# One pass over quarter slices for the statistics and the recurrence input, and a normalized input that is recomputed instead of spilled

## The chip, the cores and the metric

The kernel runs on the 8 cores of one Trainium2 chip. Each core works on its own half of one of four sequences, and no core talks to another. The metric is the device time of the slowest core, in microseconds. The chip has two dies, with cores 0 to 3 and 4 to 7.

## What is computed

One layer on x of shape (4, 4096, 2048): a layer norm, a linear recurrence with 256 complex states, a gated feed-forward block that a router switches per token, and a residual.

```python
xn = _layernorm(x, axis=-1)                       # (x - mean) / sqrt(var + 1e-5)
# recurrence on xn:
Bu_re = jnp.einsum('btd,nd->btn', x, gB_re)       # the same for Bu_im
new_re = A_re * h_re - A_im * h_im + bu_re        # scan over t, complex A
y = einsum(H_re, C_re) - einsum(H_im, C_im) + D * x
# block on xn:
routed = jax.nn.sigmoid(x @ w_router + b_router) > 0.5
h = x + (rmsnorm(x, norm1_w) @ wv + bv) @ wo
h2 = rmsnorm(h, norm2_w)
mlp = (silu(h2 @ w_gate) * (h2 @ w_up)) @ w_down
g = silu(where(routed, h + mlp, x))
out = x + y * g
```

D = 2048, FF = 5632. A core has T = 2048 tokens of its own (`xT`, transposed: features are rows, tokens are columns) and a second block of 2048 tokens (`xNB`), the first half of its sequence. From `xNB` it needs only the state at the end of the recurrence, as the start value for its own half (times zero for cores that own a first half).

## The kernel before

Everything is laid out with 128 features or states in the partitions and tokens along the free axis. A feature dimension of 2048 is NK = 16 tiles. The program is written out by hand for five engines: `prog[e]` is the order in which engine e runs, `wait` puts a semaphore wait into it, `milestone` a drain that counts its engine's semaphore up, and `fence` makes engines wait for all others and for all DMA semaphores. `op` puts a drain between every two instructions of VectorE, ScalarE and GpSimd. All x tiles are loaded, and all spills stored, by the DMA queue of SyncE, in program order; the weights are loaded by GpSimd's.

The stages, in order (`pmark` names them):

- P0a: small parameters, and the rotation table `R_bf`, built by doubling on VectorE.
- P0stats_own, P0stats_nb: `stats_pass` loads 16 tiles of 128x2048, casts each on VectorE, squares it on ScalarE, and sums over features with one-column matmuls (weights `ones_bf`, or `sw_sb`, two columns in f32 that also give the router's sum). Then row arithmetic on one partition (mean, variance, `Sqrt`, `reciprocal`), and `bcast`, a matmul with `ones1` that spreads a row over 128 partitions, four quarters each, through banks 6 and 7. The own pass also makes `rr1_bc` and the router's `mask_bc`.
- P0bu_nb, P0bu_own: `bu_pass` loads x again in two halves of 1024 columns, casts on VectorE, and multiplies with `bcat_sb` into four planes of two banks each. Then it applies mean and scale on VectorE. `rotate_scan` rotates the planes by `R_bf` (six tensor operations for each of NG = 2 groups) and runs `tensor_tensor_scan` over 2048 columns. For `xNB` this follows at once; for the own tokens it is `lru_tail_own`, which is called after phase3(0), with the copy into `g_bf`.
- Then, for each half s of the own tokens (1024 columns): `phase3` (x again, `h1_pl`, then v = h1 wv), `phase4` (v wo plus the normalized x gives h, the second norm), `phase5` (gate and up, FFC = 44 steps), `phase6` (down, y, and the output).

In phase4 each of 16 steps d loads `xb4` (one buffer), subtracts `m_bc` and multiplies by `r_bc` into `x4tmp`, stores `x4tmp` to `xnspill` by SyncE's queue, and adds the result of 32 matmuls into `h_pl[d]`. In phase6 each of 16 steps d has two quarters q; each loads h, x and the spilled normalized x (`xn_b`), and VectorE's epilogue runs after the step's matmuls.

The few lines on which most hangs, in `phase4`:

```python
if d >= 1:
    wait("sync", sV, mk_xc[d - 1])
mk_x = dma("sync", sX[0], xb4, xT[d * 128:(d + 1) * 128, c0:c0 + TS])
...
wait("vector", sO, sO.v)
mk_xc[d] = tt("vector", x4tmp, xb4, m_bc[:, c0:c0 + TS], AL.subtract, inc=sV)
mk_xn = tt("vector", x4tmp, x4tmp, r_bc[:, c0:c0 + TS], AL.mult, inc=sV)
wait("sync", sV, mk_xn)
dma("sync", sO, xnsp[d * 128:(d + 1) * 128, c0:c0 + TS], x4tmp)
```

## Time and profile before

| | us |
|---|---|
| two timed runs | 3749.3 and 3793.7, median 3771.5 |
| the profiled execution, device time | 3763.05 |
| its span on the slowest core (core 7) | 3761.5 |
| spans of the other cores | 3733.1 to 3757.8 |

The profile is that of core 7. Its times start at the span's start. The stages of core 7 lie, by the first DMA or the first instruction of each, at 0 to 738 (all of P0), 738 to 928 (phase3(0)), 928 to 1150 (phase4(0)), 1150 to 1778 (phase5(0)), 1778 to 2249 (phase6(0)), 2249 to 2440, 2440 to 2662, 2662 to 3289 and 3289 to the end (the same four for s = 1). TensorE is busy for 73% of the span, VectorE 29%, ScalarE 10%, GpSimd 10%. Busy means an instruction on the engine; the table of stages gives also the granted clock of TensorE (1.00 is 2.4 GHz, 0.50 is 1.2 GHz) and the share of time in which the 16 DMA engines moved data.

### The profile page before, as it was taken

To read this page: it belongs to the slowest core of one execution; us is meant where nothing else is said; L and a number is where in the kernel's file an instruction comes from. 1 tells how busy PE (TensorE), PEld (TensorE's weight loads), DVE (VectorE), ACT (ScalarE), POOL (GpSimd) and SP (SyncE) were. 2 spreads that over 40 slices of the span, in tenths; PEclk is the share of its full clock that TensorE was granted. 3 is DMA by queue.
4 is the path that set the end of the run, shared out by engine and by line. 5 is a ranking of instruction groups with operands and counts; after the bars stand their busy time and mean duration, and the time that the engine had idled before them with its cause. 6 is when DMAs were issued, how large, how long until landed. Compare 5 with 4: busy or idle time off the path is not lost.

```text
span 3761.5 us, 31591 instructions; the slowest of 8 cores (3733.1 to 3761.5 us)
## 1 busy us (share of the span) xinstructions
PE 2757.8 (73%) x11800; PEld 1166.7 (31%) x11800; DVE 1084.0 (29%) x1391; ACT 382.1 (10%) x459; POOL 363.6 (10%) x311
## 2 busy tenths in 40 slices
PE   0635533348856999998688874885599999968887
PEld 0101211113312444444233331332244444423333
DVE  5363455571341101101232333034211010123222
ACT  0212000021111000000000002101200000000000
POOL 0000000001101111111010100110111111101000
PEclk6857676769977999999888986998799999989998
DMA  2404222457957777776787774695777887688876
GB/s 46 142 37 152 92 91 89 111 101 76 153 123 119 79 75 74 76 79 65 122 131 134 124 125 101 69 153 113 135 74 77 79 78 75 63 128 127 138 116 116
DMA packets 749608, 381.71 MB, mean 101 GB/s; under 512 B 684930, under 2 KB 686994, under 8 KB 745362
## 3 DMA queue, kind: packets, MB, share of 16 engines
q0 software_dynamic: 679728, 178.28, 48.8%
q1 hardware_dynamic: 69730, 201.42, 17.0%
q8 instruction: 96, 1.57, 0.2%
q14 instruction: 54, 0.44, 0.0%
HBM read 507.56 MB, written 50.33 MB: 148 GB/s over the span
## 4 chain that ended last, share of the span: by engine, by line
PE 51%; DMA 26%; DVE 14%; issue 4%; ACT 2%; PEld 1%; DVEq 1%; PEldq 1%; SPq 0%; POOL 0%; ACTq 0%; POOLq 0%
PE ps L153 51%; DMA arena<-down_p 9%; DMA arena<-xT 9%; DVE arena L157 7%; DMA arena<-xNB 3%; DVE arena L177 2%; DMA arena<-wv_p 2%; ACT arena L174 2%; DMA arena<-up_p 1%; PEld ps L153 1%; DVE arena L161 1%; PEldq L187 1%; DVEq L121 1%; DVE arena L169 1%; DMA arena<-wo_p 1%
## 5 line engine op out<-in xcount | busy, mean ns | idle before, releaser
L153 PE MATMUL ps<-arena 128*128 128x512 bf16 x11264 | 2566.9, 390 | 691.6 <-DMA arena<-down_p 201.0
L153 PEld LDWEIGHTS ps<-arena 128*128 128x128 bf16 x11264 | 1117.1, 100 | 2143.2 <-issue 910.5
L157 DVE TENSOR_TENSOR arena<-arena,ps 128x512 bf16<-128x512 f32 (+1 forms) x304 | 208.9, 687 | 1760.4 <-ACT arena L174 1127.5
L174 ACT ACTIVATE arena<-arena 128x512 f32<-128x512 f32 (+4 forms) x135 | 146.9, 1088 | 1512.5 <-DVE arena L181 896.5
L174 ACT ACTIVATE arena<-ps 128x512 f32<-128x512 f32 x176 | 105.1, 597 | 1095.5 <-PE ps L153 1082.9
L147 POOL DMA_DIRECT2D arena<-gate_p x88 | 100.6, 1143 | 1163.5 <-PE ps L153 999.4
L157 DVE TENSOR_TENSOR arena<-arena,m_bc 128x1024 f32<-128x1024 f32 x64 | 78.4, 1225 | 423.0 <-DMA arena<-xT 382.1
L157 DVE TENSOR_TENSOR arena<-arena 128x512 f32<-128x512 f32 (+8 forms) x227 | 187.5, 826 | 33.4 <-DMA hspill<-arena 13.0
L153 PE MATMUL ps<-arena,ones_bf 128*1 128x512 bf16 x256 | 82.5, 452 | 152.2 <-ACT arena L174 120.6
L147 POOL DMA_DIRECT2D arena<-down_p x64 | 85.9, 1343 | 788.0 <-PE ps L153 788.0
L177 DVE CAST arena<-arena 128x1024 bf16<-128x1024 f32 (+1 forms) x96 | 83.7, 871 | 254.2 <-DMA arena<-xT 122.2
L147 POOL DMA_DIRECT2D arena<-wv_p x32 | 37.3, 1165 | 1081.0 <-DVEq L187 735.8
L153 PE MATMUL ps<-arena,ones 1*128 1x512 f32 x56 | 50.5, 1075 | 121.6 <-DVEq L187 84.4
L174 ACT ACTIVATE arena<-arena,vp 128x1024 bf16<-128x1024 f32 x64 | 73.4, 1148 | 495.7 <-DVE arena L157 492.5
L147 POOL DMA_DIRECT2D arena<-up_p x88 | 101.2, 1150 | 0.0
L153 PEld LDWEIGHTS ps<-arena,ones_bf 128*1 128x1 bf16 x256 | 19.6, 91 | 216.9 <-issue 209.1
L153 PE MATMUL ps<-arena,sw_sb 128*2 128x512 f32 (+1 forms) x160 | 62.1, 531 | 27.6 <-DMA arena<-xT 26.4
L169 DVE SCALAR_TENSOR_TENSOR arena<-arena,vp,ps 128x512 f32<-128x512 f32 x64 | 47.8, 747 | 59.8 <-ACT arena L174 58.8
L174 ACT ACTIVATE arena<-ps,vp 128x512 bf16<-128x512 f32 x64 | 44.0, 687 | 191.7 <-PE ps L153 186.1
L153 PEld LDWEIGHTS ps<-arena,ones 1*128 1x128 f32 x56 | 16.6, 314 | 150.5 <-issue 150.5
L147 POOL DMA_DIRECT2D arena<-wo_p x32 | 36.5, 1142 | 275.1 <-PE ps L153 243.1
L177 DVE COPY arena<-ps 128x512 f32<-128x512 f32 (+2 forms) x64 | 44.0, 688 | 40.4 <-PE ps L153 33.8
(54 smaller groups left out, 464.8 us busy)
## 6 DMA issues: line engine op xcount, KB each, us to landing
arena<-xT SPq DMA_DIRECT2D x96, 512.0 KB, 5.2
arena<-gate_p POOLq DMA_DIRECT2D x88, 512.0 KB, 7.3
arena<-up_p POOLq DMA_DIRECT2D x88, 512.0 KB, 9.1
arena<-down_p POOLq DMA_DIRECT2D x64, 704.0 KB, 9.6
arena<-xT SPq DMA_DIRECT2D x16, 1024.0 KB, 5.5
arena<-xNB SPq DMA_DIRECT2D x16, 1024.0 KB, 4.9
arena<-xNB SPq DMA_DIRECT2D x32, 512.0 KB, 4.7
arena<-wv_p POOLq DMA_DIRECT2D x32, 512.0 KB, 6.6
```

Source lines behind the costliest of these rows:

```text
L121: prog[e].append(lambda E: E.drain())
L147: return op(queue, lambda E, o=out_ap, i=in_ap: E.dma_start(out=o, in_=i), inc=sem, n=16, is_dma=True)
L153: E.matmul(o, l, r, start=a, stop=b), inc=inc)
L157: E.tensor_tensor(o, a, b, al), inc=inc)
L161: E.tensor_single_scalar(o, a, s, al), inc=inc)
L169: E.scalar_tensor_tensor(o, a, s, b, o0, o1), inc=inc)
L174: E.activation(o, i, f, bias=b, scale=s), inc=inc)
L177: return op(e, lambda E, o=out_ap, i=in_ap: E.tensor_copy(o, i), inc=inc)
L187: em(e, lambda E, h=s.h: E.drain().then_inc(h, 1))
```

## The change

The two statistics passes and the two bu passes over x become one `fused_pass` for `xNB` and one for the own tokens. Each goes over four quarters q of 512 columns; a quarter has 16 steps k. A step loads 128x512 (two buffers), casts and squares on ScalarE, and runs on TensorE: the sum with one f32 column of `sw_sb` (bank 4), for own tokens a second one for the router (bank 6), the sum of squares (bank 5), and four matmuls with `bcat_sb` into banks 0 to 3. After the 16 steps comes the quarter's row arithmetic, now over 512 columns, with `bcq`, a spread through bank 7 alone; ScalarE copies the four planes from PSUM; VectorE applies mean and scale, rotates, and scans, with the last column kept in `small` as the start value of the next quarter. For own tokens ScalarE copies the four results into `g_bf` at each quarter's end. `lru_tail_own` is gone. The order is now xNB first, then own.

In phase4 the store to `xnspill` and its two waits are gone, and the normalized x is made in `h_pl[d]` in place. In phase6 the two loads of it are gone, with SyncE's wait for `mk_Hc`; two tensor operations on 128x512 ahead of each epilogue make it again from the x that is loaded anyway.

The diff, cut to its core (removed bodies of functions are left out, they are printed above):

```diff
--- before.py
+++ after.py
...
-    xnsp = nc.dram_tensor("xnspill", [D, T], F32)
...
     milestone("vector")
...
-    def stats_pass(src, own):
...
-    def bcast(row_ap, dst, qn=4):
...
-    mk_ns = stats_pass(xNB.ap(), False)
...
-    def bu_pass(src, mbc, rbc, mk_ps_free):
...
-    def rotate_scan(init_cols):
...
+    xq2 = [arF(64, 512), arF(66, 512)]
+    xbfq = [arB(68, 512), arB(69, 512)]
+    xsqq = [arB(70, 512), arB(71, 512)]
+    upq = [arF(72, 512), arF(74, 512), arF(76, 512), arF(78, 512)]
...
+    def bcq(row_ap, dst_ap, mk_row):
+        wait("tensor", sV, mk_row)
+        wait("tensor", sV, st["b7"])
+        mk1 = mm(ps[7][:, :], ones1[:, :], row_ap, True, True, inc=sT)
+        wait("vector", sT, mk1)
+        st["b7"] = cp("vector", dst_ap, ps[7][:, :], inc=sV)
+        ps_rd[7] = st["b7"]
+
+    def fused_pass(src, own):
+        mbc_t = m_bc if own else mnb_bc
+        rbc_t = r_bc if own else rnb_bc
+        for q in range(4):
+            cq = q * 512
+            mkB15 = None
             for k in range(NK):
                 sl = k % 2
+                wait("sync", sT, st["S"][sl])
+                wait("sync", sS, st["c"][sl])
+                mk_x = dma("sync", sX[sl], xq2[sl],
+                           src[k * 128:(k + 1) * 128, cq:cq + 512])
+                wait("scalar", sX[sl], mk_x)
+                wait("scalar", sT, st["B"][sl])
+                st["c"][sl] = act(xbfq[sl], xq2[sl], AF.Identity, inc=sS)
+                mk_sq = act(xsqq[sl], xbfq[sl], AF.Square, inc=sS)
+                wait("tensor", sX[sl], mk_x)
+                if k == 0:
+                    wait("tensor", sSm, mk_small)
+                    wait("tensor", sV, st["ev45"])
+                st["S"][sl] = mm(ps[4][0:1, :], sw_sb[:, 2 * k:2 * k + 1],
+                                 xq2[sl], k == 0, k == NK - 1, inc=sT)
+                if own:
+                    if k == 0:
+                        wait("tensor", sV, st["s2e"])
+                        wait("tensor", sV, st["ev6"])
+                    st["S"][sl] = mm(ps[6][0:1, :],
+                                     sw_sb[:, 2 * k + 1:2 * k + 2],
+                                     xq2[sl], k == 0, k == NK - 1, inc=sT)
+                wait("tensor", sS, mk_sq)
+                if k == 0:
+                    wait("tensor", sV, st["ev5"])
+                mm(ps[5][0:1, :], ones_bf[:, :], xsqq[sl], k == 0, k == NK - 1)
+                if k == 0:
+                    wait("tensor", sBc, mk_bcat)
+                    wait("tensor", sS, st["evu"])
                 for pl in range(4):
+                    st["B"][sl] = mm(
+                        ps[pl][:, :],
+                        bcat_sb[:, k * 512 + pl * 128:k * 512 + (pl + 1) * 128],
+                        xbfq[sl][:, :], k == 0, k == NK - 1,
+                        inc=sT if pl == 3 else None)
+                if k == NK - 1:
+                    mkB15 = st["B"][sl]
+            if not own and q == 0:
+                wait("tensor", sV, mk_ones)
+                mk_bs = None
+                for pl in range(4):
+                    for k in range(NK):
+                        mk_bs = mm(ps[6][:, pl:pl + 1],
+                                   bcat_sb[:, k * 512 + pl * 128:
+                                           k * 512 + (pl + 1) * 128],
+                                   negones_bf[:, :], k == 0, k == NK - 1,
+                                   inc=sT if k == NK - 1 else None)
+                wait("vector", sT, mk_bs)
+                for di, c in enumerate((0, 2, 1, 3)):
+                    cp("vector", smc(C_BS + di), ps[6][:, c:c + 1])
+                st["bse"] = milestone("vector")
+            wait("vector", sT, mkB15)
+            st["ev45"] = cp("vector", row2[0:1, cq:cq + 512], ps[4][0:1, :],
+                            inc=sV)
+            st["ev5"] = cp("vector", row_sx2[0:1, cq:cq + 512], ps[5][0:1, :],
+                           inc=sV)
+            if own:
+                st["ev6"] = cp("vector", row_s1[0:1, cq:cq + 512],
+                               ps[6][0:1, :], inc=sV)
+            rm = row2[0:1, cq:cq + 512]
+            rs1 = row_s1[0:1, cq:cq + 512]
+            rsx = row_sx2[0:1, cq:cq + 512]
+            rt = row_tmp[0:1, cq:cq + 512]
+            ra = row_aux[0:1, cq:cq + 512]
+            tsc("vector", rm, rm, INV_D, AL.mult)
+            mk_m = milestone("vector")
+            wait("scalar", sV, mk_m)
+            mk_m2 = act(rt, rm, AF.Square, inc=sS)
+            wait("vector", sS, mk_m2)
+            stt("vector", rsx, rsx, INV_D, rt, AL.mult, AL.subtract)
+            tsc("vector", rt, rsx, 1e-5, AL.add)
+            mk_v = milestone("vector")
+            wait("scalar", sV, mk_v)
+            mk_sq2 = act(rt, rt, AF.Sqrt, inc=sS)
+            wait("vector", sS, mk_sq2)
+            op("vector", lambda E, o=rt: E.reciprocal(o, o))
+            mk_r = milestone("vector")
+            bcq(rm, mbc_t[:, cq:cq + 512], mk_m)
+            bcq(rt, rbc_t[:, cq:cq + 512], mk_r)
+            if own:
+                tsc("vector", ra, rsx, 1e-5, AL.add)
+                op("vector", lambda E, o=ra: E.reciprocal(o, o))
+                tt("vector", ra, rsx, ra, AL.mult)
+                tsc("vector", ra, ra, 1e-6, AL.add)
+                mk_v = milestone("vector")
+                wait("scalar", sV, mk_v)
+                mk_sq2 = act(ra, ra, AF.Sqrt, inc=sS)
+                wait("vector", sS, mk_sq2)
+                op("vector", lambda E, o=ra: E.reciprocal(o, o))
+                tt("vector", ra, ra, rt, AL.mult)
+                mk_rr = milestone("vector")
+                bcq(ra, rr1_bc[:, cq:cq + 512], mk_rr)
+                tsc("vector", ra, rm, small[0:1, C_S2R:C_S2R + 1], AL.mult)
+                tt("vector", ra, rs1, ra, AL.subtract)
+                tt("vector", ra, ra, rt, AL.mult)
+                tsc("vector", ra, ra, br_sb[0:1, 0:1], AL.add)
+                mk_msk = tsc("vector", ra, ra, 0.0, AL.is_gt, inc=sV)
+                bcq(ra, mask_bc[:, cq:cq + 512], mk_msk)
+            wait("scalar", sT, mkB15)
+            wait("scalar", sV, st["car"])
+            mk_ue = None
+            for di, pl in enumerate((0, 2, 1, 3)):
+                mk_ue = act(upq[di], ps[pl][:, :], AF.Identity, inc=sS)
+            st["evu"] = mk_ue
+            wait("vector", sS, mk_ue)
             for di in range(4):
+                stt("vector", upq[di], mbc_t[:, cq:cq + 512], smc(C_BS + di),
+                    upq[di], AL.mult, AL.add)
+                tt("vector", upq[di], upq[di], rbc_t[:, cq:cq + 512], AL.mult)
+            for g in range(NG):
+                Rr = R_bf[:, (2 * g) * T + cq:(2 * g) * T + cq + 512]
+                Ri = R_bf[:, (2 * g + 1) * T + cq:(2 * g + 1) * T + cq + 512]
+                ur, ui = upq[2 * g], upq[2 * g + 1]
+                tt("vector", rAq, ur, Rr, AL.mult)
+                tt("vector", rBq, ui, Ri, AL.mult)
+                tt("vector", rAq, rAq, rBq, AL.subtract)
+                tt("vector", rBq, ui, Rr, AL.mult)
+                tt("vector", ui, ur, Ri, AL.mult)
+                tt("vector", rBq, rBq, ui, AL.add)
+                magc = smc(C_MAG + g)
+                for ri, dsrc in ((0, rAq), (1, rBq)):
+                    i = 2 * g + ri
+                    if q == 0:
+                        ini = smc(C_GI + i) if own else 0.0
+                    else:
+                        ini = smc(C_CAR + i)
+                    op("vector",
+                       lambda E, o=upq[i], d1=dsrc, mc=magc, iv=ini:
+                       E.tensor_tensor_scan(o, mc.broadcast_to([128, 512]), d1,
+                                            iv, AL.mult, AL.add),
+                       inc=sV)
+                    st["car"] = cp("vector", smc(C_CAR + i),
+                                   upq[i][:, 511:512], inc=sV)
+            if own:
+                wait("scalar", sV, st["car"])
+                for i in range(4):
+                    act(g_bf[:, i * T + cq:i * T + cq + 512], upq[i],
+                        AF.Identity)
+                milestone("scalar")
+
+    pmark("P0stats_nb")
+    fused_pass(xNB.ap(), False)
     for g in range(NG):
         pre, pim = smc(28 + 2 * g), smc(28 + 2 * g + 1)
         t1 = smc(C_T1)
-        ge_r = upl[2 * g][:, T - 1:T]
-        ge_i = upl[2 * g + 1][:, T - 1:T]
+        ge_r = smc(C_CAR + 2 * g)
+        ge_i = smc(C_CAR + 2 * g + 1)
         gi_r, gi_i = smc(C_GI + 2 * g), smc(C_GI + 2 * g + 1)
         tsc("vector", gi_r, ge_r, pre, AL.mult)
         tsc("vector", t1, ge_i, pim, AL.mult)
@@ -564,15 +500,17 @@
         tsc("vector", gi_r, gi_r, cmask_sb[:, 0:1], AL.mult)
         tsc("vector", gi_i, gi_i, cmask_sb[:, 0:1], AL.mult)
     milestone("vector")
+    wait("tensor", sS, st["bse"])
+    mk_S2 = None
+    for k in range(NK):
+        mk_S2 = mm(ps[6][0:1, 0:1], sw_sb[:, 2 * k + 1:2 * k + 2], onescol,
+                   k == 0, k == NK - 1, inc=sT if k == NK - 1 else None)
+    wait("vector", sT, mk_S2)
+    st["s2e"] = cp("vector", small[0:1, C_S2R:C_S2R + 1], ps[6][0:1, 0:1],
+                   inc=sV)
 
     pmark("P0bu_own")
-    ow_free, ow_fv = bu_pass(xT.ap(), m_bc, r_bc, nb_free)
-
-    def lru_tail_own():
-        rotate_scan([smc(C_GI + i) for i in range(4)])
-        for i in range(4):
-            cp("vector", g_bf[:, i * T:(i + 1) * T], upl[i])
-        milestone("vector")
+    fused_pass(xT.ap(), True)
 
...
@@ -681,18 +617,14 @@
                                    e == 0, e == NK - 1,
                                    inc=sT if e == NK - 1 else None)
             wait("vector", sX[0], mk_x)
-            wait("vector", sO, sO.v)
-            mk_xc[d] = tt("vector", x4tmp, xb4, m_bc[:, c0:c0 + TS],
+            mk_xc[d] = tt("vector", h_pl[d], xb4, m_bc[:, c0:c0 + TS],
                           AL.subtract, inc=sV)
-            mk_xn = tt("vector", x4tmp, x4tmp, r_bc[:, c0:c0 + TS], AL.mult,
-                       inc=sV)
-            wait("sync", sV, mk_xn)
-            dma("sync", sO, xnsp[d * 128:(d + 1) * 128, c0:c0 + TS], x4tmp)
+            tt("vector", h_pl[d], h_pl[d], r_bc[:, c0:c0 + TS], AL.mult)
             wait("vector", sT, mk_grp[d])
             for q in range(2):
                 bank = (2 * d + q) % 4
                 mk_hq[2 * d + q] = tt("vector", h_pl[d][:, q * 512:(q + 1) * 512],
-                                      x4tmp[:, q * 512:(q + 1) * 512],
+                                      h_pl[d][:, q * 512:(q + 1) * 512],
                                       ps[bank][:, :], AL.add, inc=sV)
             if d >= 2:
         wait("vector", sT, mk_stq[NK - 1])
-        wait("vector", sO, sO.v)
         cp("vector", rms2_bc[0:1, 0:512], ps[4][0:1, :])
         cp("vector", rms2_bc[0:1, 512:1024], ps[5][0:1, :])
         tsc("vector", rms2_bc[0:1, :], rms2_bc[0:1, :], INV_D, AL.mult)
...
             mk_x = {}
-            mk_xn = {}
-            if d == 0:
-                wait("sync", sV, mk_Hc)
             for q in range(2):
                 mk_h[q] = dma("sync", sH[q], p6h[q],
                               hsp[d * 128:(d + 1) * 128,
@@ -854,9 +782,6 @@
                 mk_x[q] = dma("sync", sX[q], p6x[q],
                               xT[d * 128:(d + 1) * 128,
                                  c0 + q * 512:c0 + (q + 1) * 512])
-                mk_xn[q] = dma("sync", sXn[q], xn_b[q],
-                               xnsp[d * 128:(d + 1) * 128,
-                                    c0 + q * 512:c0 + (q + 1) * 512])
...
                 wait("vector", sT, mk_grp[idx])
                 wait("vector", sX[q], mk_x[q])
                 wait("vector", sH[q], mk_h[q])
-                wait("vector", sXn[q], mk_xn[q])
                 wait("vector", sOut[idx % 2], sOut[idx % 2].v)
+                tt("vector", t6a, p6x[q], m_bc[:, cc:cc + 512], AL.subtract)
+                tt("vector", t6a, t6a, r_bc[:, cc:cc + 512], AL.mult)
                 tt("vector", tb, p6h[q], ps[bankd][:, :], AL.add)
                 if idx >= 1:
                     wait("vector", sS, mk_gsil[idx - 1])
-                mk_sel = sel(t6g, mask_bc[:, cc:cc + 512], tb, xn_b[q], inc=sV)
+                mk_sel = sel(t6g, mask_bc[:, cc:cc + 512], tb, t6a, inc=sV)
                 wait("scalar", sV, mk_sel)
                 mk_gsil[idx] = act(t6g, t6g, AF.Silu, inc=sS)
                 wait("vector", sS, mk_gsil[idx])
-                stt("vector", tb, xn_b[q], vp[:, d:d + 1], ps[banky][:, :],
+                stt("vector", tb, t6a, vp[:, d:d + 1], ps[banky][:, :],
                     AL.mult, AL.add)
                 mk_g[idx] = tt("vector", tb, tb, t6g, AL.mult, inc=sV)
                 mk_ep[idx] = tt("vector", tb, tb, p6x[q], AL.add, inc=sV)
@@ -913,8 +839,6 @@
     for s in range(NSUB):
         pmark("P3_s%d" % s)
         mk_v_last = phase3(s)
-        if s == 0:
-            lru_tail_own()
         pmark("P4_s%d" % s)
         mk_h2, spill_mark, mk_pf4, mk_h2tt = phase4(s, mk_v_last)
         pmark("P5_s%d" % s)
```

## Rows read from the trace of the kernel before

**Rows 1.** Busy time by stage: length, busy us (instructions) of each engine, PEclk, DMA share, GB/s.

```profile
0.00:738.00 738.00, 298.53 (x976) 94.77 (x976) 371.75 (x549) 79.47 (x54) 1.48 (x5) 0.71 0.30 94
```

**Rows 2.** Timeline, P0: end of the rotation table on VectorE; first load of phase3(0).

```profile
115.39 0.15 DVE L161 TENSOR_SCALAR small<-small 128x1 f32<-128x1 f32 x1
...
738.19 19.71 SPq L147 DMA_DIRECT2D arena<-xT  x5
```

**Rows 3.** Timeline of VectorE in phase3(0): first and last of the own recurrence's 11 rows.

```profile
811.21 4.66 DVE L157 TENSOR_TENSOR arena<-arena,R_bf 128x2048 f32<-128x2048 f32 x2
...
857.92 5.13 DVE L177 CAST g_bf<-arena 128x2048 bf16<-128x2048 f32 x4
```

**Rows 4.** Groups of instructions by form: count | busy us, mean ns | idle before.

```profile
L157 DVE TENSOR_TENSOR arena<-arena 128x512 f32<-128x512 f32 x132 | 91.4, 692 | 12.4 <-issue 1.8
...
L174 ACT ACTIVATE arena<-arena 128x512 f32<-128x512 f32 x64 | 40.3, 630 | 896.5 <-DVE arena L181 896.5
...
L543 DVE TENSOR_TENSOR_SCAN arena<-small,arena 128x2048 f32<-128x2048 f32 x8 | 35.6, 4454 | 0.7
...
L727 DVE RECIPROCAL arena<-arena 1x1024 f32<-1x1024 f32 x2 | 13.1, 6541 | 3.9 <-ACT arena L174 3.9
```

**Rows 5.** Timeline: sums at full clock in stats_own; a row spread at half clock.

```profile
127.20 3.59 PE L153 MATMUL ps<-arena,sw_sb 128*2 128x512 f32 x8 [0.84 <-DMA arena<-xT]
...
145.65 1.03 PE L153 MATMUL ps<-arena,ones_bf 128*1 128x512 bf16 x4
...
294.76 5.45 PE L153 MATMUL ps<-arena,ones 1*128 1x512 f32 x6 [9.13 <-DVEq L187]
296.90 0.69 DVE L177 CAST mask_bc<-ps 128x512 uint8<-128x512 f32 x1 [2.32 <-PE ps L153]
```

**Rows 6.** Load sizes of the whole run: KB each, median us from issue to landing.

```profile
arena<-xNB SPq DMA_DIRECT2D x32, 512.0 KB, 4.7
...
arena<-wo_p POOLq DMA_DIRECT2D x32, 512.0 KB, 8.9
xnspill<-arena SPq DMA_DIRECT2D x32, 512.0 KB, 4.5
...
out<-arena SPq DMA_DIRECT2D x64, 256.0 KB, 3.5
```

**Rows 7.** Windows of 5 us at the start of bu_nb, one of 6 us in stats_nb.

```profile
435.00:440.00 5.00, 5.00 (x20) 2.02 (x18) 1.39 (x2) 0.00 (x0) 0.00 (x0) 0.80 0.64 197
440.00:445.00 5.00, 3.57 (x16) 1.29 (x14) 1.39 (x2) 0.00 (x0) 0.00 (x0) 1.00 0.65 208
...
370.00:376.00 6.00, 2.92 (x9) 0.71 (x7) 0.88 (x1) 1.14 (x1) 0.00 (x0) 0.78 0.75 270
```

**Rows 8.** Chain of phase4: steps 1 to 15 of s = 0, with one whole step.

```profile
948.73 1.23 DVE arena L157
...
1003.54 1.23 DVE arena L157
1004.86 1.24 DVE arena L157
1006.16 0.33 SPq L147
...
1006.53 7.45 DMA arena<-xT
...
1096.74 1.23 DVE arena L157
```

**Rows 9.** The same chain for s = 1, first and last.

```profile
2464.14 1.22 DVE arena L157
...
2606.19 1.23 DVE arena L157
```

**Rows 10.** Timeline of phase6(0): GpSimd's load of down weights, and TensorE's restart on it.

```profile
1907.82 1.34 POOL L147 DMA_DIRECT2D arena<-down_p  x1 [20.33 <-PE ps L153]
...
1917.14 23.18 PE L153 MATMUL ps<-arena 128*128 128x512 bf16 x96 [4.25 <-DMA arena<-down_p]
```

More of the change, by code:

```diff
@@ L426, in build_nc @@
-    wait("tensor", sV, mk_msk)
-    bcast(row_tmp[0:1, :], mask_bc)
-    pmark("P0stats_nb")
-    fence(("tensor",))
-    mk_ns = stats_pass(xNB.ap(), False)
-    wait("vector", sT, mk_ns)
-    for q in range(4):
-        cp("vector", row2[0:1, q * 512:(q + 1) * 512], ps[q][0:1, :])
-    for q in range(4):
-        cp("vector", row_sx2[0:1, q * 512:(q + 1) * 512], ps[4 + q][0:1, :])
-    tsc("vector", rowm, rowm, INV_D, AL.mult)
-    mk_m = milestone("vector")
-    wait("scalar", sV, mk_m)
-    mk_m2 = act(row_tmp[0:1, :], rowm, AF.Square, inc=sS)
@@ L441, in build_nc @@
-    wait("vector", sS, mk_m2)
-    stt("vector", row_sx2[0:1, :], row_sx2[0:1, :], INV_D, row_tmp[0:1, :],
-        AL.mult, AL.subtract)
-    tsc("vector", row_sx2[0:1, :], row_sx2[0:1, :], 1e-5, AL.add)
-    mk_v = milestone("vector")
-    wait("scalar", sV, mk_v)
-    mk_sq = act(row_sx2[0:1, :], row_sx2[0:1, :], AF.Sqrt, inc=sS)
-    wait("vector", sS, mk_sq)
-    op("vector", lambda E: E.reciprocal(row_sx2[0:1, :], row_sx2[0:1, :]))
-    mk_rnb = milestone("vector")
+    row_aux = arF(40, T)
```

210 lines of the change are left out of this document (12 added, 198 removed).

## Prediction

> **What bounds the kernel now.** I read the table of stages first, then the chain of waits stage by stage. In P0, 738 us long, no engine is near its bound: TensorE is busy 299 us, VectorE 372, ScalarE 79, the DMA engines 30% [rows 1]. It is a row of latencies: the rotation table holds VectorE until 115.5 us, then come four passes over x, with row arithmetic on one partition between them, and phase3's first load goes out at 738.2 [rows 2]. The own tokens' rotation and scan do not lie there: VectorE runs them from 811 to 863 us, under the wv matmuls [rows 3], so they cost nothing now. Phase4 is a loop of one load, two VectorE operations and the store's issue: from the first to the fifteenth of its steps 148.0 us pass, 10.57 each, in the second half 142.05 us, 10.15 each [rows 8, 9]. Phase5 is TensorE's own and untouched. In phase6 TensorE waits 4.25 us per step for the down weights, whose load was issued 9.3 us earlier [rows 10]; VectorE's epilogue is off the path.
>
> **The parts of P0.** The new P0 is a sum of streams (16 steps of loads and matmuls) and tails (what follows a quarter).
>
> *TensorE in a step.* At full clock a pass over 128x512 in f32 costs 3.59/4 = 0.86 us (its eight records start 0.43 apart to the one-column bf16 pass behind them) and a bf16 one 0.216 (1.03 for four, the last one's drain in it) [rows 5]. xNB: 0.86 + 5 x 0.216 = 1.94. Own: 2 x 0.86 + 1.08 = 2.80. At half clock twice that: 3.9 and 5.6.
>
> *The load.* Two buffers, each free again when the last f32 pass has read it. No row has a lone load of 128x512. A 512 KB load lands in 4.7 us; the 512 KB store took 4.5 and the 256 KB one 3.5 [rows 6]. So halving the size takes off between 0 and 1.0: 3.7 to 4.7, and no less than 3.5. I take 4.0, nearer to the pair of stores. Adding 0.3 for semaphores and the f32 passes (0.86, or 1.72 own), a buffer's cycle is 5.2 us for xNB and 6.05 own, and two buffers give 2.6 and 3.03 us a step. ScalarE's cast and square are 2 x 0.7 from 0.63 [rows 4]; the step's bf16 work waits for them: 0.15 + 1.4 + 1.08 = 2.6, the same for xNB, hidden own. With 3.5 the steps are 2.4 and 2.8 (TensorE's bound), with 4.7 they are 2.95 and 3.38.
>
> The Trainium skill, DMA: Bandwidth & Descriptors, section Anatomy of one DMA, fits a transfer by 2.0 us and bytes over 436 GB/s, which is an estimated 2.6 us here. The steps would then be 2.1 and 2.8, P0 some 34 us shorter. The trace disagrees for 512 KB: 3.2 by the page, 4.7 measured [rows 6].
>
> *The clock.* After idleness TensorE is at half clock; in bu_nb it was busy throughout 435 to 440 at a mean of 0.80 and then at 1.00, while busy 3.57 of 5 us [rows 7]. I charge two steps of each stream at half clock. Streams: xNB 14 x 2.6 + 2 x 3.9 = 44.2; own 14 x 3.03 + 2 x 5.6 = 53.6, less the f32 pass that is done ahead: 52.
>
> *The tail.* A VectorE operation on 512 columns is 0.69, 0.77 with its drain; a scan 4.45/4, so 1.25; `reciprocal` 6.54/2, so 3.35 with its milestone; ScalarE 0.63 and 0.1 [rows 4]. A spread is 2.14 us from matmul to copy at half clock, and 0.8 for the copy [rows 5]; with one bank they follow one another. xNB, until TensorE gets to the next quarter's first pass (the spreads stand ahead of it in its queue): two copies 1.5, scaling 0.6, `Square` 0.8, two row operations 1.4, `Sqrt` 0.75, `reciprocal` 3.5, copy 0.8, matmul 1.75: 11.1. VectorE goes on for 1.2 (second copy), 20 operations (15.4), 4 scans (5) and 4 small copies (1), 34 in all, but beside the next stream of 44.2: hidden, and it costs 23 us only behind the last quarter.
>
> Own tokens have no such cover. The mask's spread stands in TensorE's queue, and the copies into `g_bf` stand in ScalarE's queue ahead of the next quarter's first cast, waiting for this quarter's scans. So the whole tail is exposed: 13.1 as for xNB with a third copy, two more reciprocals 6.8, `Sqrt` 0.9, nine row operations 5.7, two spreads 5.9: 32.4. Then 21.4 of rotation and scan, and 2.9 for four copies: 56.7 us, in which TensorE idles. This is where rows 3's 52 us come to: off a covered place, onto the path.
>
> *The sum.* xNB's first quarter streams under the rotation table (16 x 3.9 = 62 us from about 26 us, when Bcat is there). Tail from 115.5, with 1.1 for the column sums: TensorE is free at 127.7. Three streams and two gaps: 3 x 44.2 + 2 x 11.1 = 154.8, to 282.5. Last tail 33.7 and start values 4.3: 320.5; TensorE waits for the latter, since the own router pass waits for `s2e`. Own: 4 x 52 + 4 x 56.7 = 434.8, to 755. Against 738.2 that is +17, though x is read twice instead of four times: 115 + 205 for xNB, 435 own.
>
> **Phase4.** The load's issue moves up from 1006.53 to behind the subtraction (1003.54 + 1.23 + 0.08): 1.68 us per step [rows 8]. 28 such steps: -47. The multiplication then hides under the load. The store's 512 KB no longer run beside the load, whose landing here (7.45 in the row shown) is over the 4.7 of elsewhere [rows 6]; I take off 0.3 a step, -8. What is late next: TensorE needs 34 x 0.216 = 7.3 a step [rows 5], and the wo load, 8.9 us [rows 6] on two buffers with 6.9 of matmuls, sets (8.9 + 6.9)/2 = 7.9. The load loop falls to 10.36 - 1.98 = 8.4, just above. So -55; bounds -30 (loads that land later because the three streams crowd) and -69 (floor 7.9).
>
> **Phase6.** Two operations of 0.77 come ahead of each epilogue, 1.54 us. Between epilogues VectorE idles, since TensorE's group takes longer than the epilogue, and SyncE's loads of the next step still land before their group ends. It costs only where nothing follows: at the ends of both phases, +3. The two loads that go were issued after the down weights on which TensorE waits, and in time they land behind them, so they free nothing there. SyncE's loads at the phase's start no longer wait for `mk_Hc`; TensorE waits there for weights anyway: 0.
>
> Sum: 3763 + 17 - 55 + 3 = 3728, against the profiled 3763.05. That execution lies 0.2% under the median of the two runs shown, 3771.5; I leave it so.
>
> **Rivals.**
> 1. *Crowded or slow small loads.* 256 KB lands like 512 KB, in 4.7. Then the 42 full-clock xNB steps cost 0.35 more and the 56 own ones 0.35: +34, 3762. For it: the 512 KB loads land in 4.7 though the DMA engines were busy only 0.65 of the time [rows 7], so it isn't the bytes alone that set it. Against: the stores' pair.
> 2. *Everything fast.* Load 3.5 (-9 and -13) and phase4 at its floor (-14): 3692. For it: half the bytes of before are in flight in P0. Against: no load of the size landed in 3.5 in the rows. The page's 2.6 us, a sentence apart, would make this 3680.
> 3. *The clock stays down in the streams.* This ends on the other side. TensorE's steps hold waits, for the load and for ScalarE, and each tail sends it back to half clock. If it stays there, a step costs 3.9 and 5.6: 42 x 1.3 + 56 x 2.57 = +199, 3927. It decides once more than a fifth of the steps run at half (40 us). For it: in stats_nb the clock was 0.78 while TensorE was busy 2.92 of 6 us. Against: bu_nb at 3.57 of 5 held 1.00 [rows 7], and the new streams have 1.94 of 2.6 and 2.80 of 3.03. The Trainium skill, TensorE: Matmul & The Clock Gate, section on HAM oscillation, tells of a kernel that falls back to half clock in each wait between bursts; the tails here are such waits and are charged, the steps I hold not to be.
> 4. *Own tail costs less*, as ScalarE would not be held by the scans. The order of the queues in the diff excludes it.
>
> **Chances.** Forecast (3705 to 3750) 0.52, rival 1 (3750 to 3790) 0.20, rival 2 (3675 to 3705) 0.18, rival 3 and mixtures with it (above 3790) 0.10. The point is the forecast's, 3728. The range leaves out rival 3 and the lower edge of rival 2: 3682 to 3795. Over 2% faster means under 3696 and over 2% slower means over 3847, against 3771.5; two per cent is about what a measurement here tells from no change. Rival 2's better part and the noise of the baseline give 0.17 faster, part of rival 3 gives 0.07 slower, 0.76 lie between.
>
> **What would show it.** In the profile after: phase3's first load at about 755 us; own quarters 109 us apart, each with 57 us in which TensorE does only spreads; xNB quarters 55 apart; steps of 2.6 and 3.0 us; granted clock 1.00 within streams; small loads near 4.0 us; phase4's steps at 8.4 us instead of 10.4; phase6 as before and 1.5 us later at its end. I am wrong if the streams' clock is below 1, if small loads take over 4.7, or if phase4's steps stay above 9.

## The result and the profile after

| | us |
|---|---|
| the profiled execution of the changed kernel, device time | 3689.9 |
| its span on the slowest core (core 2) | 3688.4 |
| spans of the other cores | 3657.9 to 3688.3 |
| ratio to the kernel before | 0.9807, 95% interval 0.9765 to 0.9849 |

The changed kernel is 1.9% faster: by its ratio, 3690 us against 3762.6 (the median of ten executions of the kernel before). The forecast was 3728. About half of the changed kernel's eleven executions were disturbed (the cores of a die at a lower granted clock), which is why the median of them all is 3823.7; the ratio leaves those out, and what follows leaves such cores out, so that the stages of the kernel with the store alone are those of its cores 4 to 7, and phase6 of the kernel with the spill alone taken away is that of its cores 0 to 3.

Stage lengths are the median over the eight cores (a stage begins with GpSimd's first weight load in it). The rows of before that were shown are core 7's, so it stands beside.

| | P0 | ph3(0) | ph4(0) | ph5(0) | ph6(0) | ph3(1) | ph4(1) | ph5(1) | ph6(1) |
|---|---|---|---|---|---|---|---|---|---|
| before | 734.7 | 188.1 | 230.6 | 622.8 | 466.8 | 185.1 | 222.9 | 623.5 | 466.7 |
| before, core 7 | 738.7 | 189.5 | 222.1 | 628.5 | 471.2 | 190.2 | 221.6 | 626.5 | 473.1 |
| after | 748.5 | 186.6 | 184.4 | 623.5 | 470.1 | 184.2 | 187.9 | 623.0 | 467.1 |
| after, core 7 | 750.9 | 186.1 | 185.3 | 626.1 | 474.8 | 189.9 | 190.7 | 622.1 | 461.0 |

P0 cost 13.8 us (forecast 17), phase6 3.3 and 0.4 (forecast 3 in all), and phase4 gave back 46.2 and 35.0, 81 together (forecast 55, bound 69). The forecast's miss lies in phase4.

First the view by windows of the changed kernel, all of P0 and the best part of phase4(0), against [rows 1] and [rows 8]. Columns: stretch, length, busy time of PE, PEld, DVE, ACT, POOL with counts, granted clock, DMA share, GB/s.

```profile
0.00:752.00 752.00, 409.37 (x1168) 87.46 (x1168) 350.61 (x658) 211.70 (x341) 1.48 (x5) 0.76 0.20 48
...
950.00:1076.00 126.00, 122.17 (x532) 50.48 (x531) 57.37 (x60) 15.86 (x15) 15.98 (x14) 0.96 0.79 119
```

In P0 no engine is near its bound, as before. In phase4 TensorE now is: 122 of 126 us. The chain of waits through phase4(0) of the changed kernel (start, length, what), where [rows 8] had load, VectorE, issue, load:

```profile
958.53 9.27 DMA arena<-wo_p
968.05 25.07 PE ps L150 x100
...
1016.76 45.27 PE ps L150 x204
...
1076.99 0.69 DVE arena L154
```

In this chain and the later ones pieces under 0.3 us are left out. After two weight loads at the start, of which the second is shown, the chain stays with TensorE to the last step, but for one 0.7 us of VectorE. 204 matmuls are six steps of 34, so a step takes 45.27/6 = 7.55 us, where the load loop's took 10.15 to 10.57. The loads of the changed kernel, from its list of DMA issues (size, median us to landing over the whole program, to be held against [rows 6]):

```profile
arena<-xT SPq DMA_DIRECT2D x128, 256.0 KB, 3.7
arena<-xT SPq DMA_DIRECT2D x64, 512.0 KB, 5.3
arena<-xNB SPq DMA_DIRECT2D x64, 256.0 KB, 3.2
...
arena<-wo_p POOLq DMA_DIRECT2D x32, 512.0 KB, 6.9
```

The weight load of wo lands in 6.9 us and not in 8.9 as before. The forecast held that number fixed; it is where phase4 went past it.

The timeline of P0's own part in the changed kernel (start, busy time, engine, operation, and in brackets the idle time before it and who ended it; TensorE's weight loads are left out here and below):

```profile
371.01 2.22 DVE L174 COPY arena<-ps 1x512 f32<-1x512 f32 x3 [49.65 <-PE ps L150]
...
425.76 2.72 ACT L171 ACTIVATE g_bf<-arena 128x512 bf16<-128x512 f32 x4 [32.85 <-DVE small L174]
428.63 2.76 ACT L171 ACTIVATE arena<-arena 128x512 bf16<-128x512 f32 x4 [0.15 <-issue]
430.12 0.59 PE L150 MATMUL ps<-arena,ones_bf 128*1 128x512 bf16 x1 [23.90 <-ACT arena L171]
...
436.54 1.88 PE L150 MATMUL ps<-arena,sw_sb 128*1 128x512 f32 x4
438.25 0.38 PE L150 MATMUL ps<-arena,ones_bf 128*1 128x512 bf16 x1
438.56 1.04 PE L150 MATMUL ps<-arena 128*128 128x512 bf16 x4
...
439.53 1.88 PE L150 MATMUL ps<-arena,sw_sb 128*1 128x512 f32 x4
...
587.20 2.22 DVE L174 COPY arena<-ps 1x512 f32<-1x512 f32 x3 [53.73 <-PE ps L150]
...
694.32 2.22 DVE L174 COPY arena<-ps 1x512 f32<-1x512 f32 x3 [52.44 <-PE ps L150]
```

The tail runs from 371.01 to the first square's matmul at 430.12, and ScalarE's four copies into `g_bf` wait 32.85 us for the scans, with the next quarter's casts behind them. The rows from 436.54 to 439.53 are one step of the stream, 2.99 us. The rows 371.01, 587.20 and 694.32 begin the tails of quarters 0, 2 and 3, about 108 us apart (forecast 109); phase3's first x load is issued at 751.9 (forecast 755).

### The profile page after: what moved, and what is told of

It is laid out like the page before. It is cut to its first block, busy times and chain, and to the rows that moved or that the text cites. A ratio compares the mean times of both kernels' runs of the same rounds, so it can differ in the third digit from the quotient of the medians.

```text
span 3688.4 us, 33165 instructions; the slowest of 8 cores (3657.9 to 3688.4 us)
## 1 busy us (share of the span) xinstructions
PE 2854.7 (77%) x11992; PEld 1156.6 (31%) x11992; DVE 1101.4 (30%) x1608; ACT 514.2 (14%) x746; POOL 362.7 (10%) x311
## 4 chain that ended last, share of the span: by engine, by line
PE 59%; DMA 16%; DVE 12%; issue 6%; PEld 3%; ACT 3%; PEldq 1%; DVEq 1%; ACTq 0%; POOL 0%; SPq 0%; POOLq 0%
PE ps L150 59%; DMA arena<-down_p 9%; DVE arena L154 5%; PEld ps L150 3%; ACT arena L171 2%; DMA arena<-wv_p 2%; DVE arena L158 1%; DMA arena<-xNB 1%; DMA arena<-wo_p 1%; DMA arena<-up_p 1%; DMA hspill<-arena 1%; PEldq L184 1%; DVE arena L421 1%; DVEq L118 1%; DVE arena L474 1%
## 5 line engine op out<-in xcount | busy, mean ns | idle before, releaser
L150 PEld LDWEIGHTS ps<-arena 128*128 128x128 bf16 x11264 | 1104.6, 100 | 1942.5 <-issue 715.6
L171 ACT ACTIVATE arena<-arena 128x512 bf16<-128x512 f32 (+4 forms) x374 | 249.9, 668 | 1521.5 <-DVE arena L178 888.1
L154 DVE TENSOR_TENSOR arena<-arena,m_bc 128x512 f32<-128x512 f32 (+1 forms) x128 | 122.7, 959 | 784.3 <-PE ps L150 467.3
L171 ACT ACTIVATE arena<-ps 128x512 f32<-128x512 f32 x208 | 124.2, 597 | 1099.0 <-PE ps L150 1083.8
L150 PE MATMUL ps<-arena,sw_sb 128*1 128x512 f32 (+1 forms) x416 | 202.0, 598 | 44.3 <-DVE small L174 25.3
L154 DVE TENSOR_TENSOR arena<-arena 128x512 f32<-128x512 f32 (+8 forms) x272 | 196.6, 723 | 38.1 <-DMA hspill<-arena 16.1
L150 PE MATMUL ps<-arena,ones_bf 128*1 128x512 bf16 x192 | 69.7, 392 | 98.9 <-ACT arena L171 98.5
L144 POOL DMA_DIRECT2D arena<-wv_p x32 | 36.5, 1142 | 1092.8 <-ACTq L184 749.5
L174 DVE COPY arena<-ps 1x512 f32<-1x512 f32 (+1 forms) x36 | 24.6, 683 | 294.1 <-PE ps L150 289.8
L154 DVE TENSOR_TENSOR arena<-arena,r_bc 128x512 f32<-128x512 f32 (+1 forms) x112 | 94.6, 845 | 9.3 <-issue 0.4
L150 PEld LDWEIGHTS ps<-arena,sw_sb 128*1 128x1 f32 x416 | 23.3, 82 | 159.6 <-issue 159.6
L150 PEld LDWEIGHTS ps<-arena,ones_bf 128*1 128x1 bf16 x192 | 13.7, 83 | 188.5 <-issue 187.9
```

Source lines behind the costliest of these rows:

```text
L144: return op(queue, lambda E, o=out_ap, i=in_ap: E.dma_start(out=o, in_=i), inc=sem, n=16, is_dma=True)
L150: E.matmul(o, l, r, start=a, stop=b), inc=inc)
L154: E.tensor_tensor(o, a, b, al), inc=inc)
L171: E.activation(o, i, f, bias=b, scale=s), inc=inc)
L174: return op(e, lambda E, o=out_ap, i=in_ap: E.tensor_copy(o, i), inc=inc)
```

## Experiments

Each was run beside the kernel before on one chip, but not all on the same chip. "P0" and "phase4" below are medians over the cores, as in the table.

### The two halves of the change

The new P0 alone, with phase4 and phase6 of before:

```diff
 # before.py
-    stats_pass, bu_pass, rotate_scan; lru_tail_own() after phase3(0)
+    fused_pass(xNB.ap(), False); fused_pass(xT.ap(), True)
```

> Only P0 is changed (one fused pass each for xNB and own tokens); phase4 and phase6 are those of before, with the spill. If the two parts of the change don't touch each other: P0 about 748 us on the median core against 735 before (+14), phase4 231 and 223 as before, total +14 us, ratio about 1.004. If P0's lighter traffic or the missing recurrence under phase3 helped later stages: phase3 or phase5 shorter by several us and the total not slower than before.

Measured: ratio 1.0059 (1.0022 to 1.0097). P0 749.5, phase4 224.6 and 224.4, phase6 470.0 and 468.6. The new P0 makes the kernel slower by 0.6%.

Only the hunks of phase4 and phase6, on the P0 of before:

```diff
 # before.py, phase4
-    wait("sync", sV, mk_xn)
-    dma("sync", sO, xnsp[...], x4tmp)
+    # normalized x made in h_pl[d]; two tensor ops in phase6
```

> Only the spill of the normalized x is taken away (phase4 and phase6 changed), P0 is that of before. Parts independent: P0 735, phase4 about 184 and 188 on the median core instead of 231 and 223 (-81), phase6 +3 in the first half and +1 in the second, total about -78 us, ratio about 0.979. If the saving in phase4 came in part from the new P0 (cores arriving there at other times): phase4 stays over 195.

Measured: ratio 0.9841 (0.9707 to 0.9975), a wide interval; the stages are sharper: P0 736.5, phase4 185.2 and 190.3, phase6 470.3 and 468.1. Phase4's whole gain is here. What the new phase6 costs can't be told: the kernel above, which keeps the old phase6, has 470.0 and 468.6.

### Phase4: traffic or order

The change does two things there: the store's 512 KB per step are gone, and the x load is issued earlier. Three kernels make the other corners of the square. The first keeps the early issue and stores 512 KB of the mean per step. This store waits for nothing and is issued right behind the load, where the old one stood ahead of the next load:

```diff
 # after.py, phase4, behind the x load
+    dma("sync", sO, xnsp[d*128:(d+1)*128, c0:c0+TS], m_bc[:, c0:c0+TS])
```

> The changed kernel with a 512 KB store per step of phase4 added back (the bytes of m_bc go to the scratch tensor), issued right behind the load and waited for by nobody in the loop. Theory traffic: the store's bytes were what made both loads late; x loads land in about 6.7 us instead of 5.7, wo loads in about 8.9 instead of 6.9, phase4's step goes from 7.5 to about 8.2 us, so about +20 us for 30 steps. Rival order: only the earlier issue and the multiplication under the load count; landing times and steps stay (7.5 us), total within 5 us of the changed kernel.

The second has no store, but issues the load behind the multiplication:

```diff
 # after.py, phase4
-    wait("sync", sV, mk_xc[d - 1])
+    wait("sync", sV, mk_xm[d - 1])   # mark of the multiplication
```

> The changed kernel, but phase4's next x load waits for the multiplication instead of the subtraction; no store. Theory traffic: with loads landing in 5.6 us the loop is 5.6 + 2.9 = 8.4 to 8.5 us, over TensorE's 7.5, so phase4 is longer by about 0.9 x 15 = 14 us in each half, +28 us in all. Rival order alone (landing as before, 6.7): loop 9.6, +62 us in all. If the loop is TensorE's and the load has slack: nothing.

The third has both, with the store behind the multiplication as before, but VectorE never waits for the store to land:

```diff
 # after.py, phase4: mk_xm as above, and behind the multiplication
+    wait("sync", sV, mk_xm[d])
+    dma("sync", sO, xnsp[...], m_bc[:, c0:c0+TS])
```

> The changed kernel with both halves of the old phase4 loop: a 512 KB store (of m_bc's bytes) issued behind the multiplication, and the next x load issued behind it; VectorE does not wait for the store to land, as it did before. The store alone gave 211.5 and 203.8 us for the two phase4 on the median core (184.4 and 187.9 without), the later issue alone 188.3 and 187.5, the kernel before 230.6 and 222.9. Theory (a product of the two: a late issue costs only when the load lands late): 6.7 to 7 us of landing plus 3.3 gives steps of 10 to 10.4, phase4 225 to 231 and 218 to 224, about +75 us against the changed kernel. Rival (the rest came from VectorE waiting for the store's landing): phase4 stays at 205 to 213 in both halves, +40.

Measured (phase4(0) and (1); the landings are those of phase4(0), median over the cores):

| store | issue | phase4 | x lands in | wo lands in | ratio |
|---|---|---|---|---|---|
| no | early (after) | 184.4, 187.9 | 5.85 | 7.1 | 0.9807 |
| no | late (e4) | 188.3, 187.5 | 4.75 | 7.05 | 0.9826 (0.9797 to 0.9854) |
| yes | early (e3, cores 4 to 7) | 214.0, 206.9 | 7.1 | 9.7 | 0.9954 (0.9905 to 1.0003) |
| yes | late (e9) | 226.8, 228.9 | 7.25 | 9.25 | 1.0043 (0.9997 to 1.009) |
| before | late | 230.6, 222.9 | 7.65 | 8.8 | 1 |

The chain of waits of the third row's kernel, core 4, in phase4(0):

```profile
1002.62 9.29 PE ps L151 x34
1011.93 11.56 DMA arena<-wo_p
1023.74 16.65 PE ps L151 x68
1040.40 9.96 DMA arena<-wo_p
```

and that of the kernel with both, on its slowest core, core 0:

```profile
1009.37 1.23 DVE arena L155
1010.69 1.24 DVE arena L155
1012.00 0.33 SPq L145
1012.37 11.77 DMA arena<-xT
1024.28 1.23 DVE arena L155
```

With the store alone TensorE waits for the weights. With store and late issue the chain is the load loop of before, [rows 8], and phase4 takes 455.7 us together against 453.5 before. The other two kernels that have the old phase4 took 449.0 (the new P0 alone, above) and 459.0 (the recurrence on the path, below), so 455.7 is the same as before: the two parts of the edit account for the whole of it, and VectorE's wait for the store's landing, which went too, was worth nothing that shows.

Alone, the late issue costs 4 and 0 us, not the expected 28: a load issued later also lands sooner, 4.75 instead of 5.85, and TensorE's 7.5 us per step cover the rest. The traffic alone costs 30 and 19 (expected 20 in all), and only on top of it the late issue costs another 13 and 22. Read the other way, taking away the store alone, with the issue left late, brings phase4 from 455.7 to 375.8 us, 80 of the 83; taking away the late issue alone brings 35.

The median landing of wo doesn't give the 30 by the forecast's formula: (9.7 + 6.9)/2 = 8.3 a step, 12 us in 16 steps. The loads on the chain above are longer than the median, 9.96 and 11.56 us. In phase4(0) TensorE waits 29.6 to 34.0 us for wo on cores 4 to 7, against 11.7 to 14.4 on the cores of the changed kernel, and it is busy for 131 to 136 us instead of 126 to 130, with a granted clock of 0.80 to 0.83 instead of 0.82 to 0.85. By the medians that is 19.5 and 7.2, 27 of the 30. What the store's bytes hold up on their way (the DMA engines, the memory) is not shown, nor whether 512 KB of another load would do the same.

### P0: what a tail costs, and where it may lie

The kernel before, with the own tokens' recurrence put on the path:

```diff
 # before.py
-        if s == 0: lru_tail_own()      # after phase3(0)
+    lru_tail_own()                     # end of P0
```

> The kernel before with one edit: the own tokens' rotation and scan (lru_tail_own) run at the end of P0 instead of behind phase3's vector work. Theory (that place was fully covered): P0 longer by the 52 us that it takes, no stage shorter, total +52 us, ratio 1.014. Rival (its place under phase3 cost something there, as VectorE and ScalarE share the stage): phase3 of the first half shorter by several us and less than +45 in total.

Measured: P0 784.5 (+49.8, expected 52), phase3(0) 186.4 (−1.7), ratio 1.0174 (1.0136 to 1.0213), which is 51 to 80 us; the mean span of the cores grew by 47. Timeline of core 7, first and last of its 2048-column operations:

```profile
738.53 4.66 DVE L157 TENSOR_TENSOR arena<-arena,R_bf 128x2048 f32<-128x2048 f32 x2
...
785.24 5.13 DVE L177 CAST g_bf<-arena 128x2048 bf16<-128x2048 f32 x4
```

In the kernel before this work was free under the wv matmuls [rows 3]; the change gave that up.

In the changed kernel, the `g_bf` copies moved to VectorE:

```diff
 # after.py, fused_pass, own
-    wait("scalar", sV, st["car"])
-    act(g_bf[...], upq[i], AF.Identity)      # x4, then milestone
+    st["car"] = cp("vector", g_bf[...], upq[i], inc=sV)   # x4
```

> The changed kernel with one edit: the four copies into g_bf at the end of an own quarter run on VectorE behind the scans, no longer on ScalarE, so ScalarE's next casts don't wait for the scans. Theory (the exposed tail is set by ScalarE's queue): TensorE is then held only until the mask's spread, about 32 us after a quarter's end, instead of 57; three tails shorten by about 25 us each, P0 from 748 to about 673, total about -75 us against the changed kernel, ratio to before about 0.961. Rival (VectorE's rotation and scan bound the quarter whoever copies): own quarters stay near 107 us apart and nothing is gained.

Measured: P0 668.9, ratio 0.9577 (0.9544 to 0.961). Own quarters are 81.8 us apart (367.62, 449.39, 531.28, 613.17) instead of 108. Timeline of core 3:

```profile
449.39 2.22 DVE L174 COPY arena<-ps 1x512 f32<-1x512 f32 x3 [25.08 <-PE ps L150]
468.74 2.63 ACT L171 ACTIVATE arena<-ps 128x512 f32<-128x512 f32 x4
...
471.45 2.76 ACT L171 ACTIVATE arena<-arena 128x512 bf16<-128x512 f32 x4
...
479.13 2.04 PE L150 MATMUL ps<-arena,ones 1*128 1x512 f32 x2 [4.07 <-DVE arena L158]
481.10 3.57 PE L150 MATMUL ps<-arena,sw_sb 128*1 128x512 f32 x4
```

ScalarE passes from the plane copies straight to the next casts (471.45), and what holds TensorE is now only the row arithmetic and its spreads. So rotation and scan lay on the path because of the queue of ScalarE alone: 26 us in each of three tails. The tail behind the last quarter has nothing to hide under.

Next, the whole tail cut into pieces that are issued behind steps of the next quarter's stream (the router's column sum moves into xNB's first quarter as well):

```diff
 # after.py, fused_pass
+    run_pend(k)                    # behind step k of each stream
-    row arithmetic, spreads, rotation, scans, g_bf copies in line
+    at(0, mean); at(1, variance, reciprocals); at(3, 5, spreads)
+    at(7, 9, router rows, rotation, scans); at(13, 15, g_bf copies)
```

> The changed kernel with every quarter's tail taken into the next quarter's stream: only the copies out of PSUM stand between two streams; row arithmetic, spreads, rotation, scans and g_bf copies are placed between the steps of the next quarter (the router's column sum moves to xNB's first quarter). Theory (tails are exposed only by their place in the queues): own quarters about 55 us apart instead of 107, xNB quarters about 44 to 46 instead of 54, one tail of about 45 us left behind the last own quarter, P0 about 520 to 560 us, total about -200 us, ratio to before about 0.93. Rival (the waits inside the streams hold TensorE as long as the tails did, or keep it at half clock): P0 over 650.

Measured: P0 543.6, ratio 0.9235 (0.9202 to 0.9268), 7.7% faster than the kernel before. Windows of core 4 (columns as above): one own quarter, then what follows the last.

```profile
364.00:428.00 64.00, 56.21 (x152) 11.78 (x152) 41.18 (x51) 26.93 (x43) 0.00 (x0) 0.92 0.26 66
...
490.00:543.00 53.00, 8.16 (x8) 1.99 (x8) 40.99 (x50) 6.78 (x11) 0.00 (x0) 0.50 0.00 0
```

TensorE is busy in 56 of 64 us where it idled through tails. The quarters end their streams at 304.62, 364.33, 428.15 and 489.95, 60 to 64 apart. The last tail, 53 us, stays bare. The chain of waits of the same core shows why it is 64 and not the 16 x 2.99 = 48 of the steps alone:

```profile
364.38 0.63 ACT g_bf L171
...
379.93 25.24 PE ps L150 x71
405.31 0.69 DVE mask_bc L174
...
428.19 0.63 ACT g_bf L171
```

Until 405.3 the chain is ScalarE's copies, one load of 4.27 us and TensorE's stream; then come 23 us of VectorE, which starts the rotation only behind the mask's copy. Rotation and scans placed earlier would be the next thing to try; it was not run.

### P0: buffers

Four x buffers instead of two in the streams, once on the changed kernel and once on the kernel with the pieces:

```diff
-    xq2 = [arF(64, 512), arF(66, 512)]
+    xq2 = [arF(64, 512), arF(66, 512), arF(92, 512), arF(94, 512)]
+    # four semaphores, buffer k % 4
```

> The changed kernel with four x buffers instead of two in the fused streams. The trace of the changed kernel has TensorE busy without a gap in own streams at 2.99 us a step and with gaps in xNB's. Theory (own streams are TensorE's, xNB's are the load's): own quarters unchanged, xNB quarters 3 to 8 us shorter each, P0 about -9 to -24 us. Rival, the recorded forecast (own streams are the load's too, at 3.03 against TensorE's 2.80): own quarters shorter by 3 us each as well, P0 another -12.

Measured: P0 731.0, ratio 0.9752 (0.9719 to 0.9786). Timeline of core 2, the tails of two own quarters:

```profile
458.69 2.22 DVE L175 COPY arena<-ps 1x512 f32<-1x512 f32 x3 [53.12 <-PE ps L151]
...
567.26 2.22 DVE L175 COPY arena<-ps 1x512 f32<-1x512 f32 x3 [53.77 <-PE ps L151]
```

On core 2, xNB quarters fall from 60.4, 54.5 and 51.5 to 49.8, 48.2 and 48.0 us. Own quarters stay 108 apart: their streams don't wait for loads.

> Tails in the stream (as in e7_rows_in_stream) and four x buffers. In that kernel xNB quarters are 45 us apart and own ones 62, where VectorE goes from one quarter's work to the next without idling. Theory (xNB still load-bound, own bound by VectorE): xNB quarters 2 to 4 us shorter, own unchanged, P0 about 535 instead of 544, ratio to before about 0.921. Rival (xNB bound by the waits for spreads and PSUM copies): P0 unchanged.

Measured: P0 531.5, 12 us less than with the pieces alone; the profiled execution took 3477.4 us. Its two fastest executions took 3471.0 and 3477.4 us, those of the kernel with the pieces 3480.4 and 3487.1, on another chip and without an interval, so how far it is ahead is open.

## Why the forecast was off by 38 us

**Where the miss lies.** The means over the eight cores add up, so they show the shares. P0 grew by 15.0 us (forecast 17), phase4 fell by 82.2 (forecast 55), phase6 fell by 1.4 (forecast +3), and the rest fell by 2.0 (forecast 0): 70.7 us less, where the forecast had 35. Three quarters of the miss is phase4.

**The term that failed: lighter traffic in phase4.** The forecast took 0.3 us off a step for the x load without the store beside it, and left the wo load at the 8.9 us of [rows 6], without a reason; that gave the floor (8.9 + 6.9)/2 = 7.9 and the choice of 8.4. The store delayed both queues: wo falls from 8.8 to 7.1, x from 7.65 to 5.85. With 7.1 the weights' floor is (7.1 + 6.9)/2 = 7.0, below TensorE's own 7.3, and the step becomes TensorE's, 7.55. (The 0.2 us above 7.3 are two changes between wide and narrow weights, shown under P0 below.) Nothing in the trace of before excluded this: its wo loads were all measured with the store beside them. Rival 2, "everything fast", had phase4 at 7.9 and 3692 in all; its total came true, for another reason, since its share in P0 did not.

**The order counts only under traffic.** The forecast charged 47 us to the earlier issue and 8 to the traffic. The square shows that they don't add: 30 + 19 for traffic alone, 4 + 0 for the issue alone, 42 + 41 for both. So the weight of the forecast's two terms was the wrong way round as well: without the store, the earlier issue is worth 4 us and not 47. The loop is a maximum of three (TensorE's 7.5, the weights, the load loop). Taking away the store brings it to TensorE's floor; taking away only the late issue leaves the wait for the weights.

**The slowest core was not typical of phase4.** On core 7 the two phase4 went from 222.1 and 221.6 to 185.3 and 190.7, 67.7 together, just inside the bound of 69; other cores had up to 240 before. Of the gap between 55 and 81, 13 us are the term above and 13 are that the sum was made from one core's rows. Core 7's phase3, 5 and 6 also took 19 us less together, 12 of them in phase6(1), which no edit explains and which the medians over the cores don't show: one core's stages scatter by that much between executions.

**P0 was right within 3 us, on errors that cancelled.** Small loads land sooner than the 4.0 assumed; landings of the changed kernel in 0 to 750 us, xT and xNB:

```profile
DMA to landing us min/median/max: 2.8/2.9/3.4
...
DMA to landing us min/median/max: 2.8/3.2/13.4
```

They lie even under the forecast's lower bound of 3.5. The Trainium skill, DMA: Bandwidth & Descriptors, section Anatomy of one DMA, gives an estimated 2.6 for this size, for transfers that GpSimd issues (these go by SyncE's queue); it was nearer than the choice of 4.0. It would still have led to a wrong step for own tokens, because TensorE's own work there is 2.99 us and not 2.80: in the timeline shown above the two f32 passes take 1.71 (436.54 to 438.25), the one-column bf16 pass 0.31 instead of 0.216, and the four bf16 passes 0.97 instead of 0.86.

It would be easy to put the extra 0.19 down to the change between f32 and bf16. The rows say otherwise. In the kernel before, TensorE goes from bf16 to f32 and back, both with narrow weights (one and two columns), and in the changed kernel's phase4 it goes from 128 columns to one and back, all in bf16:

```profile
130.63 1.03 PE L153 MATMUL ps<-arena,ones_bf 128*1 128x512 bf16 x4
131.50 3.60 PE L153 MATMUL ps<-arena,sw_sb 128*2 128x512 f32 x8
134.93 1.03 PE L153 MATMUL ps<-arena,ones_bf 128*1 128x512 bf16 x4
...
1024.29 7.08 PE L150 MATMUL ps<-arena 128*128 128x512 bf16 x32
1031.30 0.59 PE L150 MATMUL ps<-arena,ones_bf 128*1 128x512 bf16 x2
1031.82 7.08 PE L150 MATMUL ps<-arena 128*128 128x512 bf16 x32
```

Before, from start to start, four bf16 passes take 0.87 (4 x 0.216) and four f32 ones (eight records) 3.43 (4 x 0.86): the change of type costs nothing. In phase4, 32 passes take 7.01 where 32 x 0.216 is 6.91, and two take 0.52 where it is 0.43: the change between 128 columns of weights and one costs 0.1 us each way, with no f32 in it. That is the 0.19 of a step in P0 and the 0.2 of a step in phase4.

So the step of 3.03 was right as a number and wrong as a mechanism: not the load's cycle but TensorE sets it, as one window of the changed kernel and four buffers without effect on own quarters show:

```profile
450.00:478.00 28.00, 28.00 (x86) 6.10 (x85) 0.00 (x0) 11.33 (x18) 0.00 (x0) 1.00 0.32 85
```

xNB's quarters came out right too, 55.5 us on average for 55.3. With loads of 3.2 us the forecast's cycle gives 2.2 a step, and TensorE's own work is 0.86 + 0.31 + 0.97 = 2.14; from 187.66 to 230.88 us the 16 steps took 2.70 each. Four buffers shortened these quarters by 3.5 to 10.6 us, so waits for loads are part of the rest; how it splits further is open.

**The tail was right.** 56.7 us were forecast; from 371.01 to the next cast at 428.63 it is 57.6. TensorE starts another 1.5 us later, behind the first cast and square, which the forecast left out. That ScalarE's queue holds it (rival 4 denied) is shown by moving four copies: P0 falls by 79.6. That the recurrence had been free before is shown by putting it on the path: +49.8.

**The clock's levels were right, its price was too high.** Windows of the changed kernel, a tail, the start of an own stream, and a stretch of an xNB stream:

```profile
404.00:424.00 20.00, 2.22 (x3) 0.13 (x1) 18.06 (x26) 0.00 (x0) 0.00 (x0) 0.50 0.00 0
...
432.00:438.00 6.00, 6.00 (x15) 1.07 (x14) 0.00 (x0) 1.26 (x2) 0.00 (x0) 0.78 0.15 44
...
160.00:176.00 16.00, 12.65 (x41) 2.77 (x39) 0.00 (x0) 6.29 (x10) 0.00 (x0) 1.00 0.51 93
```

TensorE is at 0.50 (1.2 GHz) in the tail, rises within 432 to 438, and is at 1.00 in the stream. Two steps at half clock were charged, 5.1 us an own stream. From 430.12 to 478.67, where the next tail begins, 48.55 us pass; 15 steps of 2.99 and 1.28 for the four planes and the square of the first are 46.1, so the slow start costs 2.4. The cheaper stream and the longer tail nearly cancel: a quarter was forecast at 52 + 56.7 and came at 48.5 + 59.1.

Rival 3 (a clock down through the streams, 3927) did not happen. The rule cited with it (the Trainium skill, TensorE: Matmul & The Clock Gate, section on HAM oscillation), a fall to half clock in waits between bursts, agrees with the tail's 0.50. The xNB stream, whose steps have short waits (TensorE busy for 12.65 of 16 us), kept 1.00 all the same.

**Rival 1** (256 KB lands like 512 KB, 4.7) is refuted by 2.9 and 3.2.

**Phase6's 3 us can be neither confirmed nor denied by its length.** The medians moved by +3.3 and +0.4, the means by −1.4 together, and kernels with the old phase6 lie between 466.6 and 470.0. What can be seen is the timeline of the last epilogue:

```profile
3678.93 0.69 DVE L154 TENSOR_TENSOR arena<-arena,m_bc 128x512 f32<-128x512 f32 x1 [3.62 <-PE ps L150]
3679.69 0.69 DVE L154 TENSOR_TENSOR arena<-arena,r_bc 128x512 f32<-128x512 f32 x1
3680.46 0.69 DVE L154 TENSOR_TENSOR arena<-arena,ps 128x512 f32<-128x512 f32 x1
```

The two added operations stand ahead of the old first one, at 3680.46, and put it off by 1.53 us (forecast 1.54), since VectorE was idle before them.

## What to carry to other kernels

When a store leaves a loop, reprice every load that ran beside it, on all queues (here it was worth 80 us of 83 without the earlier issue), and ask what the loop's step is once the loads land sooner; a loop's price is the largest of its cycles and not a sum of the parts removed. Before moving work that hides under another engine, follow each queue it passes: four copies placed ahead of the next stream's casts put 26 us a quarter onto the path, and the same tail cut up and issued inside the stream made the whole kernel 7.7% faster than before. Take a stage's length over all cores before building a sum on the slowest core's rows.
